# Cross-attention block on one core: context products in half-array pairs, the first norm in two chunks, the last first-pair queries after the values

## The chip, the cores and the metric

The kernel runs on one core of one Trainium2 chip. The metric is the device time of one execution in microseconds, as the median of several runs. Five engines work side by side, each with its own instruction queue: TensorE (PE; its weight loads are listed as PEld), VectorE (DVE), ScalarE (ACT), GpSimd (POOL) and SyncE (SP, which here only issues transfers). Semaphores order them.

## What is computed

```python
x: (4, 1024, 256)   ctx: (4, 64, 192)   HEADS, DHEAD, INNER = 16, 64, 1024   FF_HID = 1024
h = _ln(x, g1, be1)
x = _attn(h, h, Wq1, Wk1, Wv1, Wo1, bo1) + x
h = _ln(x, g2, be2)
x = _attn(h, ctx, Wq2, Wk2, Wv2, Wo2, bo2) + x
h = _ln(x, g3, be3)
y = h @ Wp + bp
a, gate = y[..., :FF_HID], y[..., FF_HID:]
out = a * gelu(gate) @ W2 + b2 + x
```

`_ln` is a normalization of each row by its mean and variance, then a scale g and a shift b. `_attn` is softmax attention with 16 heads and a scale of 1/8. All is float32.

## The kernel before

The code writes each engine's program by hand, in order; each instruction waits for semaphores that the other engines raise. No scheduler moves anything.

**The long part.** 64 steps C, each one pair of heads and one chunk of 512 queries: scores (L509, L513), exponential on ScalarE (L1161), sums of probabilities on GpSimd (L1406), values times probabilities (L526), and between them the next step's first scores (L483) with their maxima on VectorE (L833). Behind it come the cross-attention and the feed-forward part. None of it is touched, but everything must wait for the opening.

**The opening**, up to the first score at 62.26 us, in TensorE's order:

1. small matmuls that keep it busy (`rouse`), and the context turned by four transposes (`context_turn`);
2. 16 context products (L401), n = 0 to 15: eight for the cross keys, eight for the cross values, each for one pair of heads. The context has 192 features, so each product is two matmuls: 128 features, and the remaining 64, which are padded with zeros to 128 partitions (VectorE's memsets, L954 and L955). Six banks of PSUM (`CTX_BANKS`) go round; ScalarE copies each product out (L1114);
3. Wq2 turned (L414), copied out half by ScalarE (L1119) and half by VectorE (L819);
4. the first 512 rows of the first norm turned, `turn_norm((1, 0))` (L362);
5. eight key folds (`fold_keys`, L428), one for each pair of heads, each four matmuls with 64 rows of weights; VectorE (L812) and ScalarE (L1125) copy one head each; three pairs of banks go round;
6. the second 512 rows turned, `turn_norm((1, 1))`;
7. four projections of the first pair of heads (L457): u = 0 and 1 are keys of the first and second 512 rows, u = 2 and 3 queries of these; ScalarE (L1142) and VectorE (L827) split each into a high and a low part;
8. eight value folds (`fold_values`, L444), with two first scores behind each, copied by ScalarE (L1134);
9. eight value projections (L469), the transpose of the maxima (L493), and two projections of the second pair of heads.

**The first norm.** VectorE takes the statistics of eight tiles of 128 rows (L743, L745) once x is there; ScalarE takes the root (L1054), queued between its copies of products 11 and 12; VectorE inverts it (L753) and writes four tiles of normalized rows into `xn` (L764), copies its half of the turned Wq2, and writes the other four tiles when TensorE has turned the first. A chunk is turned in two halves k = 0, 1, through banks T0 and T1. ScalarE reads each half twice: into `hT`, rounded (L1102), and back into the bank in full (L1106); VectorE subtracts the two (L794), which frees the bank.

**Transfers.** SyncE issues all of them in one queue: context, weights Wk2 and Wv2 in four pieces of two transfers (L1564, L1565), x (L1525), Wq2 (L1567), the first pair's weights (L1530), six small vectors (L1570), then Wo2 and the rest.

## Time and profile before

| | us |
|---|---|
| median of 3 runs | 2023.52 (2023.45 to 2024.98) |
| the profiled execution | 2023.83 |
| its span | 2022.0 |
| PE busy | 2015.6 (100%) |
| GpSimd busy | 1476.4 (73%) |
| VectorE busy | 1390.4 (69%) |
| ScalarE busy | 1187.8 (59%) |
| first score of the long part starts | 62.26 |

The span runs from the first instruction to the last; the execution's own time has 1.8 us more around it. A timeline row gives start, time, engine, line, operation, what is written and read, and how many instructions are merged in it. A float32 matmul stands in the records as two instructions, so 16 records are 8 matmuls. TensorE's records overlap: one is listed some tenths of a us longer than the distance to the next.

### The profile page before, as it was taken

Reading aid. Unit: us, or ns where it says so; the run is one execution under the profiler, and the core shown is the slowest. Engines: PE = TensorE matmul, PEld = TensorE weight load, DVE = VectorE, ACT = ScalarE, POOL = GpSimd, SP = SyncE. Lnnn points to the kernel's source line nnn. Section 1 sums busy time; section 2 is a strip of 40 time slices with the busy share of each in tenths; the row PEclk is TensorE's granted clock in tenths of the full one; section 3 lists DMA queues with packets and bytes.
Section 4 is the critical chain, followed back from the end, with each engine's and each line's share of the span. In section 5 each row is a group of like instructions: output and inputs, shape, how many; then the busy total and the mean of one; then the engine's idle time right before and its main releaser. Section 6 shows DMA issues by size and latency. Waiting matters only on the chain.

```text
span 2022.0 us, 32384 instructions
## 1 busy us (share of the span) xinstructions
PE 2015.6 (100%) x12718; PEld 1386.8 (69%) x12718; DVE 1390.4 (69%) x2128; ACT 1187.8 (59%) x1895; POOL 1476.4 (73%) x785
## 2 busy tenths in 40 slices
PE   9999999999999999999999999999999999999999
PEld 8665665667565566765665666565558999888888
DVE  6587677666767785577678566758777888744443
ACT  6566576565557675565667555557665666533332
POOL 2699899978989998899899888989895576300000
PEclk9999999999999999999999999999999999999999
DMA  7300000001000000010000001000020520000100
GB/s 241 115 27 21 6 7 16 6 27 48 17 11 6 16 7 27 1 64 6 6 6 22 27 1 51 8 27 1 22 55 9 147 84 1 1 21 22 42 11 32
DMA packets 48183, 64.01 MB, mean 32 GB/s; under 512 B 6048, under 2 KB 41504, under 8 KB 46368
## 3 DMA queue, kind: packets, MB, share of 16 engines
q1 hardware_dynamic: 48032, 61.96, 9.7%
q8 instruction: 100, 1.64, 0.3%
q14 instruction: 51, 0.42, 0.1%
HBM read 43.07 MB, written 18.87 MB: 31 GB/s over the span
## 4 chain that ended last, share of the span: by engine, by line
PE 99%; ACT 0%; DMA 0%; issue 0%; DVE 0%; SPq 0%
PE score L526 22%; PE score L509 19%; PE score L652 9%; PE score L513 6%; PE score L457 5%; PE attn_project L637 5%; PE attn_project L666 5%; PE score L607 4%; PE attn_project L457 4%; PE first_score L483 4%; PE score L469 3%; PE score L575 2%; PE attn_project L575 2%; PE attn_project L483 2%; PE first_score L550 2%; PE attn_project L469 1%
## 5 line engine op out<-in xcount | busy, mean ns | idle before, releaser
L1406 POOL TENSOR_TENSOR acc<-acc,pT 128x1024 f32<-128x1024 f32 x384 | 916.9, 2388 | 53.8 <-POOL acc L1406 0.4
L1161 ACT ACTIVATE pT<-score 128x1024 f32<-128x1024 f32 x512 | 525.7, 1027 | 134.4 <-PE score L513 92.8
L509 PE MATMUL score<-qk 64*128 64x512 f32 x3072 | 456.6, 399 | 1.5 <-ACT oT L1174 0.9
L526 PE MATMUL score<-pT,vT 128*64 128x512 f32 x2016 | 446.5, 595 | 0.0
L833 DVE TENSOR_REDUCE nmax<-first_score 128x1 f32<-128x512 f32 x512 | 347.7, 679 | 4.8 <-PE first_score L483 2.9
L833 DVE TENSOR_REDUCE nmax<-attn_project 128x1 f32<-128x512 f32 x512 | 346.9, 678 | 0.0
L509 PEld LDWEIGHTS score<-qk 64*128 64x128 f32 x3072 | 257.3, 184 | 119.0 <-ACT pT L1161 67.9
L526 PEld LDWEIGHTS score<-pT,vT 128*64 128x64 f32 x2016 | 139.2, 137 | 289.4 <-issue 251.8
L855 DVE RECIPROCAL sums<-sums 128x512 f32<-128x512 f32 (+1 forms) x65 | 214.4, 3299 | 54.3 <-ACT sums L1207 53.7
L513 PE MATMUL score<-shift,pick 64*128 64x512 f32 x1024 | 205.5, 391 | 0.0
L483 PE MATMUL first_score<-qk 64*128 64x512 f32 x512 | 200.8, 392 | 0.0
L483 PE MATMUL attn_project<-qk 64*128 64x512 f32 x512 | 200.6, 392 | 0.0
L1403 POOL TENSOR_TENSOR acc<-pT 128x1024 f32<-128x1024 f32 x64 | 153.4, 2396 | 55.8 <-ACT pT L1161 55.8
L652 PE MATMUL score<-hT,wp 128*128 128x512 f32 x768 | 184.1, 396 | 0.0
L1393 POOL TENSOR_TENSOR xres<-xres,rows 128x1024 f32<-128x1024 f32 x8 | 19.2, 2399 | 203.1 <-DVE xn L764 203.1
L652 PEld LDWEIGHTS score<-hT,wp 128*128 128x128 f32 x768 | 142.3, 188 | 32.0
L1174 ACT COPY oT<-score 128x512 f32<-128x512 f32 x63 | 37.1, 588 | 212.1 <-PE score L526 211.9
L827 DVE SCALAR_TENSOR_TENSOR qk<-score,qk 128x512 fp32r<-128x512 f32 x67 | 46.1, 690 | 154.3 <-ACT qk L1142 154.3
L1207 ACT COPY sums<-first_score 32x512 f32<-32x512 f32 x248 | 143.1, 577 | 9.2 <-PE first_score L550 6.3
L1432 POOL TENSOR_TENSOR probs<-probs,rsum 128x1024 f32<-128x1024 f32 x32 | 61.0, 1906 | 90.8 <-DVE rsum L896 90.8
L848 DVE TENSOR_TENSOR shift<-first_score,mask 128x512 fp32r<-128x512 f32 x64 | 44.2, 691 | 116.9 <-PE first_score L493 116.9
L513 PEld LDWEIGHTS score<-shift,pick 64*128 64x128 f32 x1024 | 99.3, 184 | 21.2
(180 smaller groups left out, 3089.2 us busy)
## 6 DMA issues: line engine op xcount, KB each, us to landing
xres<-x_middle SPq DMA_DIRECT2D x10, 512.0 KB, 3.7
xres<-in_x SPq DMA_DIRECT2D x4, 1024.0 KB, 6.8
raw_qk<-in_L_xattn_Wq SPq DMA_DIRECT2D x32, 128.0 KB, 2.3
raw_qk<-in_L_xattn_Wk SPq DMA_DIRECT2D x32, 128.0 KB, 2.4
raw_v<-in_L_xattn_Wv SPq DMA_DIRECT2D x8, 512.0 KB, 3.9
keys_all<-keys SPq DMA_DIRECT2D x1, 4096.0 KB, 13.0
values_all<-values SPq DMA_DIRECT2D x1, 4096.0 KB, 12.4
out_x<-xres SPq DMA_DIRECT2D x7, 512.0 KB, 3.0
```

Of the source, the lines that this page charges most:

```text
L457: last = e.matmul(banks[bank], wqk[:, P % 2, w, kind, k, :], hT[:, h, k, c * BANK:(c + 1) * BANK], start=(i == k == 0), stop=(i == 2 and k ...
L483: last = e.matmul(banks[bank], qk[P % 2][r, w, q0:q0 + PART], qk[P % 2][r, 2 + h, half * BANK:(half + 1) * BANK], start=(m == 0), stop=(m ...
L509: e.matmul(bank, qk[P % 2][r, 2 + h, keys], qk[P % 2][r, w, queries], start=(part == 0), stop=False)
L513: e.matmul(bank, pick[r, :], shift[r, :], start=False, stop=True).then_inc(s.scored, 1)
L526: last = e.matmul(banks[bank][head * DH:(head + 1) * DH, :], vT[:, v_slot(D, jt), c0:c0 + DH], pT[:, jt, head, :], start=(jt == 0), stop=( ...
L652: last = e.matmul(banks[bank], wp[q][:, w, k, which, o:o + PART], hT[:, h, k, (c % 2) * BANK:(c % 2 + 1) * BANK], start=(term == k == 0), ...
L833: e.tensor_reduce(nmax[:, head, t, half:half + 1], banks[PASS_BANKS[head][half]], AX.X, ALU.max, negate=True).then_inc(s.row_max, 1)
L855: e.reciprocal(sums[:, C % 2, part], sums[:, C % 2, part]).then_inc(s.sum_inverse, len(halves))
L1161: e.activation(pT[:, jt].rearrange("p h n -> p (h n)"), SC[R % 2][:, :], ACT.Exp).then_inc(s.exponential, 1)
L1207: last = e.copy(sums[r * DH // 2:(r + 1) * DH // 2, o, :], banks[bank][g * DH // 2:(g + 1) * DH // 2, :])
L1403: e.tensor_tensor(total, pT[:, jt - 1], pT[:, jt], ALU.add).then_inc(s.probs_added, 1)
L1406: e.tensor_tensor(total, total, pT[:, jt], ALU.add).then_inc(s.probs_added, 1)
```

## The change

Three things, all in the opening.

**Context products in pairs.** The remaining 64 features of both keys' and values' weights are now loaded into two halves of the partitions (`wkv2_rest`: heads pairs 0 and 1 of each four on partitions 0 to 63, pairs 2 and 3 on 64 to 127). The turned context's remaining features are copied a second time, by ScalarE, to partitions 64 to 127. A group of four products makes four first parts and then four second parts with 64 rows each, which lie alternately in the lower and the upper half of the array. The order of the pairs within four is 0, 2, 1, 3. VectorE's two memsets are gone.

**The first norm by chunks.** x is loaded in two halves, the first between Wk2 and Wv2, the second behind Wv2 and g1, be1, which are moved up. Each half has statistics, a root, an inverse and rows of its own. The first chunk is turned before the last group of products, the second before the fourth key fold.

**The last queries of the first pair** (u = 3) are projected behind the value projections and the turned maxima, through another bank.

```diff
@@ the order of products @@
+        CTX_ORDER = [(i, TPC * half + p) for i in range(2) for half in range(PAIRS // TPC) for p in (0, 2, 1, 3)]
+        ctx_of = numbered(CTX_ORDER)
@@ TensorE @@
-            def context_product(n):
...
-                for k in range(2):
-                    last = e.matmul(banks[bank][:, 0:B * M], wkv2[:, i, k, p * PART:(p + 1) * PART], ctxT[:, k, :, :],
-                                    start=(k == 0), stop=(k == 1))
+            def context_products(g):
+
                 need.wait_ge(s.ctx_copied, 4)
-                need.wait_ge(s.padded, 2)
...
+                need.wait_ge(s.ctx_copied_a, 2)
+                need.wait_ge(wkv2_loaded[g], 32)
+                for n in range(4 * g, 4 * g + 4):
+                    i, p = CTX_ORDER[n]
+                    bank = CTX_BANKS[n % 6]
+                    bank_free(bank)
+                    e.matmul(banks[bank][:, 0:B * M], wkv2[:, i, p * PART:(p + 1) * PART], ctxT[:, 0, :, :],
+                             start=True, stop=False)
+                for n in range(4 * g, 4 * g + 4):
+                    i, p = CTX_ORDER[n]
+                    bank = CTX_BANKS[n % 6]
+                    r = slice(n % 2 * CREST, (n % 2 + 1) * CREST)
+                    c = p // TPC * BANK // 2 + p % 2 * PART
+                    e.matmul(banks[bank][:, 0:B * M], wkv2_rest[r, i, c:c + PART], ctxT[r, 1, :, :],
+                             start=False, stop=True).then_inc(s.ctx_product, 1)
+                    free[bank] = ((s.kv2_a, n + 1),)
...
-            for n in range(2 * PAIRS):
-                context_product(n)
+            for g in range(4):
+                context_products(g)
+                if g == 2:
+                    turn_norm((1, 0))
             turn_wq2()
-            turn_norm((1, 0))
             for p in range(PAIRS):
+                if p == 3:
+                    turn_norm((1, 1))
                 fold_keys(p)
-            turn_norm((1, 1))
-            for u, bank in zip((0, 2, 1, 3), CTX_BANKS):
+            for u, bank in zip((0, 2, 1), CTX_BANKS):
                 project_qk(0, u, bank)
...
             turn_max(0, "T1")
+            project_qk(0, 3, "PJ")
@@ VectorE @@
-            e.memset(wkv2[CREST:PART, :, 1, :], 0.0).then_inc(s.padded, 1)
-            e.memset(ctxT[CREST:PART, 1, :, :], 0.0).then_inc(s.padded, 1)
             context_turn()
-            for t in range(TILES):
+            for t in range(TPC):
                 stats1(0, t)
-            ln_inverse(rs1[:, :], (1, 0))
+            ln_inverse(rs1[:, 0:TPC], (1, 0))
             norm1(0)
+            for t in range(TPC, TILES):
+                stats1(0, t)
+            turn_half((1, 0), 0, "T0")
+            ln_inverse(rs1[:, TPC:], (1, B))
+            norm1(1)
             turn_wq2()
-            norm1(1)
             for p in range(PAIRS):
                 fold_keys(p)
-                if p == 3:
-                    turn_norm((1, 0))
+                if p == 1:
+                    turn_half((1, 0), 1, "T1")
             turn_norm((1, 1))
...
             make_shift(0, "T1")
+            split_qk(0, 3, "PJ")
@@ ScalarE @@
+            def context_turn():
+
+                bpt = PART // M
+                for a in range(2):
+
+                    need.wait_ge(s.ctx_copied, 2 * a + 2)
+                    e.copy(ctxT[CREST:PART, 1, a * bpt:(a + 1) * bpt, :],
+                           banks[TURN_BANKS[2 * a + 1]][0:CREST, 0:PART].rearrange("p (b m) -> p b m", b=bpt)
+                           ).then_inc(s.ctx_copied_a, 1)
...
+            context_turn()
             for n in range(2 * PAIRS):
                 context_product(n)
-                if n == TILES + 3:
-                    ln_root(mv1[:, :, 1], (1, 0), (1, TILES - 1))
+                if n == 5:
+                    ln_root(mv1[:, 0:TPC, 1], (1, 0), (1, TPC - 1))
+                if n == 11:
+                    turn_half((1, 0), 0, "T0")
+                if n == 13:
+                    ln_root(mv1[:, TPC:, 1], (1, B), (1, TILES - 1))
             turn_wq2()
+            turn_half((1, 0), 1, "T1")
             for p in range(PAIRS):
-                if p < KT:
-                    turn_half((1, 0), p, ("T0", "T1")[p])
+                if 4 <= p < 4 + KT:
+                    turn_half((1, 1), p - 4, ("T0", "T1")[p - 4])
                 fold_keys(p)
-            turn_norm((1, 1))
-            for u, bank in zip((0, 2, 1, 3), CTX_BANKS):
+            for u, bank in zip((0, 2, 1), CTX_BANKS):
                 split_qk(0, u, bank)
...
+            split_qk(0, 3, "PJ")
@@ GpSimd @@
-            need.wait_ge(*rows_there((1, 0)))
+            need.wait_ge(*rows_there((1, 1)))
             split_wqk(0)
-            need.wait_ge(*rows_there((1, 1)))
             split_wv(0)
@@ SyncE @@
-                    e.dma_start(wkv2[:, i, 0, part], w[0:PART, part]).then_inc(there, 16)
-                    e.dma_start(wkv2[0:CREST, i, 1, part], w[PART:CD, part]).then_inc(there, 16)
-            load_x(0)
+                    rest = slice(half * INNER // 4, (half + 1) * INNER // 4)
+                    e.dma_start(wkv2[:, i, part], w[0:PART, part]).then_inc(there, 16)
+                    e.dma_start(wkv2_rest[:, i, rest], w[PART:CD, part].rearrange("r (g n) -> g r n", g=2)
+                                ).then_inc(there, 16)
+                if i == 0:
+                    load_x_first(0)
+            for c, v in enumerate((g1, be1)):
+                load_cols(c, v, s.cols1_loaded)
+            load_x_first(1)
             e.dma_start(wq2[:, :, :], Wq2.rearrange("(k p) n -> p k n", p=PART)).then_inc(s.wq2_loaded, 16)
             load_wqk(0)
```

How rows move. First TensorE, from the first context product to the first key folds. Before:

```order
L401 MATMUL score0<-ctxT,wkv2 128x256 x4
L401 MATMUL score1<-ctxT,wkv2 128x256 x4
L414 MATMUL attn_project<-ident,wq2 128x128 x8
L414 MATMUL score0<-ident,wq2 128x128 x8
L362 MATMUL first_score<-ident,xn 128x128 x8
L428 MATMUL score0<-kv2,wq2T 128x256 x4
L428 MATMUL score1<-kv2,wq2T 128x256 x4
L428 MATMUL attn_project<-kv2,wq2T 128x256 x4
```

And in the changed kernel, from the third group of products on:

```order
L409 MATMUL score1<-ctxT,wkv2 128x256 x2
L409 MATMUL attn_project<-ctxT,wkv2 128x256 x2
L416 MATMUL score1<-ctxT,wkv2_rest 128x256 x2
L416 MATMUL attn_project<-ctxT,wkv2_rest 128x256 x2
L369 MATMUL first_score<-ident,xn 128x128 x8
L409 MATMUL score0<-ctxT,wkv2 128x256 x2
L409 MATMUL score1<-ctxT,wkv2 128x256 x2
L416 MATMUL score0<-ctxT,wkv2_rest 128x256 x2
L416 MATMUL score1<-ctxT,wkv2_rest 128x256 x2
L428 MATMUL attn_project<-ident,wq2 128x128 x8
L428 MATMUL score0<-ident,wq2 128x128 x8
L442 MATMUL score0<-kv2,wq2T 128x256 x4
```

The turn of the norm's rows (`first_score<-ident,xn`) moved from between Wq2's turn and the key folds to before the last group.

Second VectorE, from the end of the statistics to the first key copies. Before:

```order
L753 RECIPROCAL rs<-sd 128x8
L764 TENSOR_SCALAR xn<-xres,mv,rs 128x256 x4
L819 COPY wq2T<-attn_project 128x4x128
L819 COPY wq2T<-score 128x4x128
L764 TENSOR_SCALAR xn<-xres,mv,rs 128x256 x4
L812 TENSOR_SCALAR keys<-score 128x8x64 x2
```

In the changed kernel:

```order
L814 TENSOR_TENSOR hT<-first_score,hT 128x512
L773 RECIPROCAL rs<-sd 128x4
L784 TENSOR_SCALAR xn<-xres,mv,rs 128x256 x4
L839 COPY wq2T<-attn_project 128x4x128
L839 COPY wq2T<-score 128x4x128
L832 TENSOR_SCALAR keys<-score 128x8x64 x2
L814 TENSOR_TENSOR hT<-first_score,hT 128x512
```

The copies of the turned Wq2 now stand behind the rows of the second chunk, and these behind the second inverse.

Third ScalarE, from the copies of the last products to the projections' first splits. Before:

```order
L1054 ACTIVATE sd<-mv,eps 128x8
L1114 COPY kv<-score 128x256 x4
L1119 COPY wq2T<-attn_project 128x4x128
L1119 COPY wq2T<-score 128x4x128
L1102 ACTIVATE hT<-first_score,cols 128x512
L1106 ACTIVATE first_score<-first_score,cols 128x512
L1125 ACTIVATE keys<-score 128x8x64
L1102 ACTIVATE hT<-first_score,cols 128x512
L1106 ACTIVATE first_score<-first_score,cols 128x512
```

In the changed kernel:

```order
L1148 COPY kv<-score 128x256 x2
L1076 ACTIVATE sd<-mv,eps 128x4
L1148 COPY kv<-score 128x256 x2
L1153 COPY wq2T<-attn_project 128x4x128
L1153 COPY wq2T<-score 128x4x128
L1125 ACTIVATE hT<-first_score,cols 128x512
L1129 ACTIVATE first_score<-first_score,cols 128x512
L1159 ACTIVATE keys<-score 128x8x64 x2
L1159 ACTIVATE keys<-attn_project 128x8x64
L1159 ACTIVATE keys<-score 128x8x64
L1125 ACTIVATE hT<-first_score,cols 128x512
L1129 ACTIVATE first_score<-first_score,cols 128x512
```

The root of the second chunk stands two product copies later than the one root before, and the two halves of a chunk's turn now stand among the later key copies.

## Rows read from the trace of the kernel before

**Rows 1.** The page: busy time, and the chain that ended last.

```profile
PE 2015.6 (100%) x12718; PEld 1386.8 (69%) x12718; DVE 1390.4 (69%) x2128; ACT 1187.8 (59%) x1895; POOL 1476.4 (73%) x785
...
PE 99%; ACT 0%; DMA 0%; issue 0%; DVE 0%; SPq 0%
```

**Rows 2.** Stretches: us, each engine's busy us, granted clock, DMA share, GB/s.

```profile
30.00:35.00 5.00, 4.25 (x25) 3.08 (x21) 2.47 (x5) 4.67 (x8) 5.00 (x8) 1.00 0.74 315
...
100.00:125.00 25.00, 25.00 (x164) 14.90 (x164) 19.34 (x26) 17.63 (x24) 23.91 (x12) 1.00 0.04 11
```

**Rows 3.** Timeline (start, time, engine, line, what): TensorE's products, Wq2's turn, value projections.

```profile
5.42 4.37 PE L401 MATMUL score<-ctxT,wkv 128*128 128x256 f32 x16 [0.22 <-DMA wkv<-in_L_xattn_Wk]
...
9.63 1.89 PE L401 MATMUL attn_project<-ctxT,wkv 128*128 128x256 f32 x8
...
19.99 1.04 PE L414 MATMUL attn_project<-ident,wq 128*128 128x128 f32 x8
...
47.96 11.46 PE L469 MATMUL score<-wv,hT 128*128 128x512 f32 x48
```

**Rows 4.** Timeline: TensorE at changes between whole-array and half-array matmuls.

```profile
27.59 1.06 PE L428 MATMUL attn_project<-kv,wq2T 64*128 64x256 f32 x8
...
28.46 1.92 PE L428 MATMUL score<-kv,wq2T 64*128 64x256 f32 x16
...
30.31 0.86 PEld L362 LDWEIGHTS first_score<-ident,xn 128*128 128x128 f32 x8 [0.33 <-issue]
30.31 1.09 PE L362 MATMUL first_score<-ident,xn 128*128 128x128 f32 x8
...
34.95 3.05 PE L457 MATMUL score<-hT,wqk 128*128 128x512 f32 x12 [0.75 <-issue]
...
37.93 1.13 PE L444 MATMUL score<-wo,kv 64*128 64x256 f32 x8
```

**Rows 5.** Timeline: from the root to the first key fold.

```profile
18.14 0.30 ACT L1054 ACTIVATE sd<-mv,eps 128x8 f32<-128x8 f32 x1 [1.03 <-DVE mv L745]
...
18.35 0.63 ACT L1114 COPY kv<-score 128x256 f32<-128x256 f32 x2
...
18.47 0.20 DVE L753 RECIPROCAL rs<-sd 128x8 f32<-128x8 f32 x1 [0.37 <-ACT sd L1054]
...
18.71 1.38 DVE L764 TENSOR_SCALAR xn<-xres,mv,rs 128x256 f32<-128x256 f32 x4
...
21.94 0.69 DVE L819 COPY wq2T<-score 128x512 f32<-128x512 f32 x1 [0.18 <-PE score L414]
...
22.78 2.00 PE L428 MATMUL score<-kv,wq2T 64*128 64x256 f32 x16
```

**Rows 6.** Timeline: ScalarE's turns and key copies, the last split, the second value fold.

```profile
22.38 0.78 ACT L1102 ACTIVATE hT<-first_score,cols 128x512 fp32r<-128x512 f32 x1 [0.29 <-PE first_score L362]
...
23.19 0.75 ACT L1106 ACTIVATE first_score<-first_score,cols 128x512 f32<-128x512 f32 x1
...
26.40 0.60 ACT L1125 ACTIVATE keys<-attn_project 128x512 f32<-128x512 f32 x1
...
26.88 0.61 ACT L1125 ACTIVATE keys<-score 128x512 f32<-128x512 f32 x1
...
36.63 0.60 ACT L1142 ACTIVATE qk<-score 128x512 fp32r<-128x512 f32 x1 [1.57 <-PE score L457]
...
37.27 0.69 DVE L827 SCALAR_TENSOR_TENSOR qk<-score,qk 128x512 fp32r<-128x512 f32 x1 [1.22 <-ACT qk L1142]
...
39.50 1.10 PE L444 MATMUL score<-wo,kv 64*128 64x256 f32 x7 [0.20 <-DVE qk L827]
```

**Rows 7.** Timeline of x and Wq2; last a transfer issue: count, KB, us to landing.

```profile
6.42 0.74 SPq L1567 DMA_DIRECT2D wq<-in_L_xattn_Wq  x1
...
13.77 0.43 DVE L743 BATCH_NORM_STATS2 stats<-xres 128x6 f32<-128x256 f32 x1 [9.08 <-DMA xres<-in_x]
...
wq<-in_L_xattn_Wq SPq DMA_DIRECT2D x1, 1024.0 KB, 10.0
```

More of the change, by code:

```diff
@@ L422, in fold_keys @@
                 need.wait_ge(s.wq2T_in_v, KT)
-                need.wait_ge(s.kv2_a, p + 1)
+                need.wait_ge(s.kv2_a, ctx_of[0, p])
                 bank_free(*fold_banks(p))
@@ L440, in fold_values @@
                     p = 2 * half + o
-                    need.wait_ge(s.kv2_a, PAIRS + p + 1)
+                    need.wait_ge(s.kv2_a, ctx_of[1, p])
                     for head, bank in enumerate(fold_banks(n % 2)):
@@ L747, in stats1 @@
             def stats1(b, t):
-                need.wait_ge(x_loaded[b % 2], 16 * (b // 2 + 1))
+                if b == 0 and t < TPC:
+                    need.wait_ge(s.x_first_loaded, 16)
+                else:
+                    need.wait_ge(x_loaded[b % 2], 16 * (b // 2 + 1))
                 ln_stats(xres[:, b % 2, t, :], mv1[:, t, :], (1, TILES * b + t))
@@ L786, in turn_half @@
                 if (key, k) in full_v:
-                    need.wait_ge(s.cols_loaded, 96)
+                    need.wait_ge(s.cols_loaded, 64)
                     which = key[0] - 1
@@ L1056, in norm_rows @@
             def norm_rows(key, src, rs, t0):
-                need.wait_ge(s.ln_negated, root_of[key[0], key[1] // CHUNKS] - 1 if key[0] == 1 else B)
+                need.wait_ge(s.ln_negated, key[1] // CHUNKS if key[0] == 1 else B)
                 need.wait_ge(s.ln_rstd, root_of[key[0], key[1] // CHUNKS])
@@ L1099, in turn_half @@
                 need.wait_ge(s.ln_turned, turned_by(key, k))
-                need.wait_ge(s.cols_loaded, 96)
+                need.wait_ge(s.cols1_loaded, 32)
+                need.wait_ge(s.cols_loaded, 64 if which else 0)
                 hT_free(key)
```

41 lines of the change are left out of this document (22 added, 19 removed).

## The prediction

> **What bounds the kernel now.** I read the busy times of the page first: TensorE is busy for 2015.6 of the span of 2022.0 us, and the chain that ended last is 99% PE [rows 1]. So an edit pays only where TensorE itself does less or waits less. The stretches show where it waits. In the long loop it doesn't, though GpSimd is nearly full there; in the opening it waits 0.75 us of one stretch [rows 2]. The diff touches only the opening, up to the first exponential at about 62 us, so the timeline of 0 to 50 us is what the sum is made from. What comes after is moved as a block. The loop has no idle time that could grow or shrink with a shift of a few us, and I cost it at nothing; if that cover is false, the price is the last rival below.
>
> The times that follow are on the clock of the profiled run. I rebuild when things happen in the new order and compare them with the old ones at two points: the first key fold (22.78 us before) and the second value fold, `fold_values(1)` (39.50 us before) [rows 5, 6].
>
> **Context products.** Between 9.63 and 19.99 us TensorE makes 12 products of two matmuls: 10.36 / 24 = 0.43 us each [rows 3]. A key fold is four matmuls with 64 rows of weights and as many columns, and starts 0.87 us after the one before it (27.59 to 28.46) [rows 4]. They run two at a time, at 0.22 us each. The eight pairs of second parts so save 8 x 0.43 = 3.46 us.
>
> Against that stands the change between whole-array and half-array matmuls, which before happens once after the products and now happens twice in each of four groups. Going in: 12 projection matmuls start at 34.95 and the value fold starts at 37.93, 2.98 us later, where 12 at the pitch of the 48 value matmuls ((11.46 - 0.16) / 48 = 0.235 us; a record ends 0.16 after the next one starts) are 2.83; the 0.15 left, with 0.07 in a slow first matmul (1.13 against 1.06 us), is 0.2 us. Going out: the sixteen records from 28.46 end their slots at 30.19 and the transposes start at 30.31, and last 1.09 instead of 1.04 us: 0.17 us [rows 3, 4]. So I take 0.37 us a group. The bounds are 0 and 0.66 (twice the 0.33 us that the weight load sat idle before 30.31 us [rows 4]); I stay with the middle value because both directions have a row of their own. A group costs 1.73 + 0.87 + 0.37 = 2.97 us instead of 3.46, and four save 2.0 us, not 3.46.
>
> The Trainium skill, "TensorEngine Tiling (Array Packing)", section Tiling Modes (Key Properties), says that changing the tiling mode drains TensorE. The overview of that page speaks of up to twice the speed for contractions of 64 or less. By the second alone the products would save 3.46 us; the rows side with the first.
>
> The first 16 records need 4.21 us where 16 need 3.46: the first three run at the lower clock [rows 3]. That costs 0.75 us and stays. The start stays at 5.42, which a weight transfer sets. ScalarE's two new copies of the turned context follow VectorE's; a 128x256 copy takes 0.37 us, and TensorE has its small warming matmuls meanwhile, so between 0 and 0.3 us are at stake; I take 0. The removed memsets of VectorE lay beside the context's loading and give nothing.
>
> So the groups end at 9.15, 12.1 and 15.1 us; the turn of norm (1, 0) follows (8 transposes, 0.88 us); the last group runs from 15.96 to 18.93; the turn of Wq2 ends at 20.7.
>
> **Are inputs there in time?** Before, all rows of x had landed at 13.77, and Wq2, issued at 6.42, 10.0 us later at 16.4 [rows 7]. Now half of x goes between the weights. From 0.5 MB in a stream of about 0.27 MB a us (1 MB of x in the 3.7 us after the weights) it costs 1.9 us of queue, so this half lands near 8.6, the second near 14.3 and Wq2 near 17.0. Four tiles' statistics take half of the 4.33 us that eight take up to 18.10: first half 10.8, second 16.5. The first half's root stands behind the copy of product 5 (12.2), its rows are ready near 14.2, 0.9 us before TensorE asks for them. Nothing waits for a transfer. SyncE queues two small g1/be1 loads ahead of Wq2, 1 us each to issue; that is in the numbers.
>
> **The new wait.** The second root is placed behind the copy of product 13 on ScalarE. That product is in the last group's first pair, done at 15.96 + 1.73 + 0.2 + 0.43, plus 0.22 to the copy = 18.54; two copies at 0.32 and the root starts at 19.17. From there before's own rows give the rest: reciprocal 0.33 later, rows 0.57 later, 1.38 long, two copies of the turned Wq2 on VectorE of 0.69, and 0.15 to TensorE [rows 5]. 19.17 + 0.57 + 1.38 + 1.38 + 0.15 = **22.65 us** for the first key fold. Before it was 22.78. TensorE is done at 20.7 and stands for 2.0 us: VectorE turns Wq2 only after it has written the second chunk's rows. Before, it wrote the first chunk's rows (18.71) there, and the second chunk's behind the copies. The queued victims are both VectorE copies and the second ScalarE half behind them. So the 2.0 us saved in the products are given back whole here, all but **0.13 us**.
>
> **From the fold to `fold_values(1)`.** Three folds end at 25.25. The turn (1, 1) is then split: its second half needs T1, which VectorE frees after two key copies (24.6 to 25.3) and a subtraction of 0.69, at 26.1. Its price is 0.3 us, plus 0.37 for changing tiles. Folds 3 to 6 run from 26.7 to 30.2. On ScalarE the turn's two halves (0.78 + 0.75, 1.57 us with gaps [rows 6]) now stand between keys 3, 4 and 5: keys 4 end at 30.5 and hold up fold 7 by 0.5 us (to 31.5). The three key copies behind them follow at 0.48 us, and free the bank of the first queries at 33.15, 0.1 after TensorE. Three projections at 1.40 end at 36.1. ScalarE's split starts 0.2 later, VectorE's 0.64 after that (36.63 to 37.27) and lasts 0.69; TensorE starts 0.14 behind it: 37.8 for `fold_values(1)` [rows 6]. Before: 39.50. What left is the stall of 0.75 us for the second chunk's turn [rows 4], the second chunk's transposes ahead of the projections (0.88, now inside the folds), and one projection (1.40). What came are the stalls above. The gain here is 1.7 us.
>
> **The fourth projection.** It is made behind the values, and costs its 1.40 us there; VectorE, idle then, hides its split. 1.7 - 1.40 = **0.3 us** at the main loop's start. Between these points the eight value folds and first scores keep their pace: they and their copies are unchanged. SyncE stores the cross keys some 2 us later (they end at 33.6 instead of about 31), still before the values' store; they have landed by about 47, the exponentials begin at 61.
>
> **Sum.** The profiled execution took 2023.83 us (span 2022.0, 1.8 around it). 2023.8 - 0.3 = 2023.5. The median shown is 2023.52, 0.3 under the profiled time, so against it the forecast is 2023.2 us.
>
> **Rivals.**
> 1. The changes of tile cost nothing. The group is 2.6 us, product 13 comes 3 x 0.37 + 0.2 = 1.3 us earlier, and so does the fold; 0.3 more goes in the folds. Gain 1.9 us, 2021.6. For it: TensorE's queue could load weights over the boundary. Against it: both boundaries show a gap [rows 4]. With every small wait of the fold stage gone too, 2020.8.
> 2. The second parts don't pair. The groups cost 0.87 more, product 13 comes 3 x 0.87 + 0.43 = 3.0 us later, **2026.2, slower**. It decides if even one of each pair waits for the other. Against it: the folds have the same alternation and are paired throughout.
> 3. The 2.0 us wait lets TensorE's clock fall. In the opening its records reach the 2.4 GHz pitch only with the fourth after 5.42, near 6.8 us (5.42 + 0.75 + 3 x 0.22) [rows 3]. If the folds had to repeat all of that, some 6 us at 1.2 GHz would cost half of them, 3.0 us: 2026.2, slower. It decides once 2.0 us of waiting is enough for the clock to fall. Against: after the gap ending at 34.95 the records are at full pitch at once [rows 4]. No row shows a gap of 2 us. The Trainium skill, "TensorE: Matmul & The Clock Gate", Part 1, says that throttled is the default state and that activity releases it; the rows of the first matmuls agree.
> 4. A transfer is late. The second half of x has 2.6 us of slack before the root, the first 0.9. Beyond that each us costs one: 2024 to 2026.
> 5. The main loop reacts to the shift, with GpSimd 96% busy in one stretch [rows 2] and first weights arriving relatively earlier; either sign, by up to 5 us.
>
> **How the numbers follow.** Forecast 2023.2 with 0.62 (own range 2022.4 to 2024.2, the upper end being tile changes of 0.66 a group). Rival 1: 0.18. Rival 2: 0.05. Rival 3: 0.05. Rival 4: 0.05. Rival 5: 0.05. The range 2020.8 to 2025.8 holds the first, rival 1, most of rival 4 and part of 5. 0.2% is 4.05 us, about what a measurement of this kernel can tell from no change; none of the first four reaches it in either direction. Same 0.92, faster 0.04, slower 0.04.
>
> **What would show it.** Right: context groups 2.9 to 3.0 us apart, half-row matmuls starting in pairs; a root near 19.2; a TensorE gap of about 2 us before the first key fold near 22.6; `fold_values(1)` near 37.8; the first score of the loop near 62.0 instead of 62.26. Wrong: a first key fold before 21.5 or after 24 us, or a loop of another length.

## The result, and the profile after

| | before | changed |
|---|---|---|
| median, us (17 runs of each, side by side) | 2025.07 (2022.95 to 2025.64) | 2027.72 (2027.28 to 2028.16) |
| the profiled execution | 2023.83 | 2027.69 |
| its span | 2022.0 | 2025.9 |

The ratio is 1.0016 [1.0009, 1.0022]: slower, by about as much as a measurement of this kernel can tell. The forecast was 2023.2, with a range up to 2025.8. The times of the kernel before fall into two groups some 2 us apart (2023.0 to 2024.0 and 2024.9 to 2026.1), so its median says mostly how many of each it caught; those of the changed kernel lie within 0.9 us. From here on I compare profiled executions, point by point. The two differ by 3.9 us.

The page of the changed kernel, against [rows 1]: TensorE has less to do, and the span is longer.

```profile
span 2025.9 us, 32389 instructions
...
PE 2014.7 (99%) x12718; PEld 1383.0 (68%) x12718; DVE 1388.9 (69%) x2127; ACT 1187.5 (59%) x1898; POOL 1477.2 (73%) x785
```

TensorE's busy time fell by 0.9 us; the rest of the span, in which it waits, rose from 6.4 to 11.2 us. The loss is in waits. Next the timeline of TensorE in the opening of the changed kernel, the answer to [rows 3 to 5] (columns as there; the bracket is the idle time before the row, and what ended it).

```profile
8.14 3.59 PE L409 MATMUL score<-ctxT,wkv 128*128 128x256 f32 x8 [3.14 <-DMA wkv_rest<-in_L_xattn_Wk]
11.66 1.13 PE L416 MATMUL score<-ctxT,wkv_rest 64*128 64x256 f32 x8
...
16.37 1.13 PE L409 MATMUL score<-ctxT,wkv 128*128 128x256 f32 x4 [0.58 <-DMA wkv_rest<-in_L_xattn_Wv]
...
19.36 1.09 PE L369 MATMUL first_score<-ident,xn 128*128 128x128 f32 x8
...
24.27 1.09 PE L428 MATMUL attn_project<-ident,wq 128*128 128x128 f32 x8 [1.01 <-DMA wq<-in_L_xattn_Wq]
...
27.25 2.00 PE L442 MATMUL score<-kv,wq2T 64*128 64x256 f32 x16 [1.02 <-DVE wq2T L839]
```

The first product starts at 8.14, where it started at 5.42 [rows 3]; three of the four brackets name a weight transfer. The rows of VectorE and ScalarE on the way to the second root, against [rows 5, 7]:

```profile
21.59 0.43 DVE L760 BATCH_NORM_STATS2 stats<-xres 128x6 f32<-128x256 f32 x1 [3.73 <-DMA xres<-in_x]
...
22.86 0.65 ACT L1148 COPY kv<-score 128x256 f32<-128x256 f32 x2 [0.65 <-PE score L416]
...
23.85 0.30 ACT L1076 ACTIVATE sd<-mv,eps 128x4 f32<-128x4 f32 x1 [0.35 <-DVE mv L762]
...
24.53 1.38 DVE L784 TENSOR_SCALAR xn<-xres,mv,rs 128x256 f32<-128x256 f32 x4
...
25.83 0.59 ACT L1153 COPY wq2T<-score 128x512 f32<-128x512 f32 x1 [0.28 <-PE score L428]
...
26.43 0.68 DVE L839 COPY wq2T<-score 128x512 f32<-128x512 f32 x1
```

VectorE stood 3.73 us for the second half of x, which was there at 21.6; the root waited for these statistics and not, as forecast, for a product's copy. From the root on the chain is the forecast one: 0.68 to the rows, 1.30 and 0.60 to the second copy, 0.82 to the fold at 27.25.

That wait is the last of three that end close together. The copies of products 12 and 13, behind which the root stands, ended at 23.51, so the root waited only 0.35 us for its statistics: the last group itself started at 20.29 where I had 15.96, as the group before it stood until 16.37 for its weights. And the turn of Wq2 stood until 24.27 for Wq2; ScalarE could copy its second half at 25.83. With x alone in time I estimate a fold 0.35 us earlier, by that wait. It was not one transfer that came late but several.

Why did x come so late? SyncE's row of issues (start, time that the issue took):

```profile
7.10 3.17 SPq L1614 DMA_DIRECT2D wkv<-in_L_xattn_Wv  x1
...
11.12 2.95 SPq L1573 DMA_DIRECT2D cols<-in_L_xattn_g  x1
...
14.81 0.66 SPq L1569 DMA_DIRECT2D xres<-in_x  x1
```

Two issues took 3 us each, where most take 0.4 to 1.6. The second half of x was issued at 14.81, half a microsecond after the time at which I had it landed. Meanwhile the 16 DMA engines had little to do. Stretches (columns as in [rows 2]):

```profile
8.00:10.00 2.00, 1.86 (x5) 1.53 (x6) 0.00 (x0) 0.00 (x0) 0.00 (x0) 0.51 0.59 196
10.00:12.00 2.00, 2.00 (x9) 1.30 (x9) 0.00 (x0) 0.00 (x0) 0.00 (x0) 0.64 0.43 159
12.00:14.00 2.00, 2.00 (x14) 1.52 (x11) 1.05 (x5) 1.20 (x4) 0.00 (x0) 1.00 0.15 51
14.00:16.00 2.00, 1.79 (x12) 0.98 (x10) 1.04 (x5) 0.61 (x3) 0.00 (x0) 1.00 0.25 48
```

The last two rows have a DMA share of 0.15 and 0.25 and some 50 GB/s, with megabytes waiting to be issued. The first two show a second thing, the granted clock at 0.51 and 0.64: TensorE fell to its lower level (1.2 GHz) at 8.0 us, and had the upper one (2.4 GHz) back at 11.45.

So there were two suspects. **Transfers**: from 13.0 us on, while a load of `wkv2_rest` runs, the trace has 23 and 24 packets of 1 KB in half a microsecond, of 47 ns each, and next to none of another transfer: 24 x 0.047 / 0.5 is the work of 2.3 engines. Such a load of 128 packets takes 128 x 0.047 / 2 = 3 us (an estimate, if two engines carry it), and four of them 12 us if it is the same two. The first and the third group wait for one, the third until 16.37 for a load issued at 6.52; SyncE's issues behind them are held up; and the first half of x, issued at 3.51, was there only 9.3 us later. **Clock**: TensorE, left idle for 3.1 us, fell to half speed, and the first group took 3.52 us for its first parts instead of 1.9.

### The profile page after: what moved, and what is told of

The parts are those of the page before. It is cut to its first block, busy times and chain, and to the rows that moved or that the text cites. A ratio compares the mean times of both kernels' runs of the same rounds, so it can differ in the third digit from the quotient of the medians.

```text
span 2025.9 us, 32389 instructions
## 1 busy us (share of the span) xinstructions
PE 2014.7 (99%) x12718; PEld 1383.0 (68%) x12718; DVE 1388.9 (69%) x2127; ACT 1187.5 (59%) x1898; POOL 1477.2 (73%) x785
## 4 chain that ended last, share of the span: by engine, by line
PE 98%; SPq 1%; ACT 0%; DMA 0%; DVE 0%; issue 0%
PE score L540 22%; PE score L523 18%; PE score L666 9%; PE score L527 6%; PE score L471 5%; PE attn_project L651 5%; PE attn_project L680 5%; PE score L621 4%; PE first_score L497 4%; PE attn_project L471 4%; PE score L483 3%; PE score L589 2%; PE attn_project L589 2%; PE attn_project L497 2%; PE first_score L564 2%; PE attn_project L483 1%
```

## The experiments

The checkpoints of every profiled execution, in us from the span's start. "Clock up" is when the records go over to the pitch of the upper level; before the first rise the records of the same matmul follow at twice the distance (0.43 instead of 0.22 us). From the loop's first score to the end it is 1959.5 to 1959.9 us in every kernel, so the loop's start says all.

| kernel | clock up | first product | first key fold | `fold_values(1)` | loop | span | ratio to before |
|---|---|---|---|---|---|---|---|
| before | 6.81 | 5.42 | 22.78 | 39.50 | 62.26 | 2022.0 | |
| before, again | 5.16 | 5.63 | 22.30 | 39.01 | 61.78 | 2021.4 | one run |
| changed | 4.62 (fell at 8.0, up again 11.45) | 8.14 | 27.25 | 42.05 | 66.23 | 2025.9 | 1.0016 |
| a_spread | 5.55 | 6.67 | 22.90 | 37.69 | 61.87 | 2021.5 | 0.9997 |
| a_rouse | up throughout | 8.01 | 27.38 | 42.18 | 66.36 | 2026.1 | 1.0015 |
| b_two | 10.56 | 7.53 | 30.42 | 47.43 | 70.20 | 2029.9 | 1.0035 |
| b_three | 9.10 | 5.79 | 24.09 | 40.80 | 63.56 | 2023.0 | 1.0006 |
| b_one | 4.96 (fell at 8.4, up again 15.20) | 9.33 | 37.71 | 54.41 | 77.18 | 2037.0 | one run |
| a_spread_wq | 4.54 | 6.81 | 22.41 | 37.19 | 61.37 | 2021.1 | 0.9998 |
| a_spread_u3 | 10.55 | 5.84 | 24.35 | 40.63 | 63.41 | 2023.0 | 1.0002 |
| b_u3 | 9.19 | 5.69 | 24.09 | 39.30 | 63.48 | 2023.1 | 0.9997 |
| a_inorder | 10.21 | 5.56 | 24.21 | 39.02 | 63.19 | 2022.9 | 0.9999 |
| a_best | 6.37 | 5.20 | 21.50 | 36.29 | 60.46 | 2020.1 | 0.9993 |

### The same data over all DMA engines (a_spread)

```diff
-                    rest = slice(half * INNER // 4, (half + 1) * INNER // 4)
                     e.dma_start(wkv2[:, i, part], w[0:PART, part]).then_inc(there, 16)
-                    e.dma_start(wkv2_rest[:, i, rest], w[PART:CD, part].rearrange("r (g n) -> g r n", g=2)
-                                ).then_inc(there, 16)
+                    if half == 0:
+                        for g in range(2):
+                            e.dma_start(wkv2_rest[g * CREST:(g + 1) * CREST, i, :].rearrange("r (h n) -> r h n", h=2),
+                                        w[PART:CD].rearrange("r (h g n) -> g r h n", h=2, g=2)[g]).then_inc(there, 16)
```

As many transfers and bytes as in the changed kernel; each now has 64 rows as its outermost size instead of 2, in packets of the same 1 KB. Both loads of a weight's rest now come with its first half, and TensorE's waits count them so.

> The changed kernel with one thing altered: the remaining 64 rows of Wk2 (and of Wv2) come in two transfers with 64 partitions outermost (each both column halves) instead of two transfers whose outermost size is 2; bytes and number of transfers are the same. Theory T (a transfer with an outermost size of 2 runs on two of the 16 DMA engines, so the first products wait for it and SyncE's queue is held up behind it): the first product starts near 6.0 us instead of 8.14, the second half of x is issued near 8 instead of 14.81 us, the first key fold starts near 23 instead of 27.25 us, fold_values(1) 14.8 us later, the first score of the loop near 62 instead of 66.23, span 2021.5 to 2022.5, 4 us under the changed kernel's 2025.9. Rival R (x's first half among the weights is what delays them): the first product stays at or after 7.5 us and the span above 2025. Rival C (the clock that fell at 8.0 us costs it): gain of at most 1.7 us.

Median 2023.36, ratio 0.9997 [0.9988, 1.0006]; span 2021.5, 4.4 us under the changed kernel's. The timeline and the stretches of a_spread:

```profile
6.67 1.97 PE L409 MATMUL score<-ctxT,wkv 128*128 128x256 f32 x8 [1.45 <-DMA wkv_rest<-in_L_xattn_Wk]
8.56 1.14 PE L416 MATMUL score<-ctxT,wkv_rest 64*128 64x256 f32 x8
...
16.53 1.89 PE L409 MATMUL score<-ctxT,wkv 128*128 128x256 f32 x8
18.36 1.13 PE L416 MATMUL score<-ctxT,wkv_rest 64*128 64x256 f32 x8
...
22.90 2.00 PE L442 MATMUL score<-kv,wq2T 64*128 64x256 f32 x16 [1.51 <-DVE wq2T L839]
```

```profile
12.00:14.00 2.00, 2.00 (x14) 1.51 (x11) 1.48 (x7) 1.38 (x5) 0.00 (x0) 1.00 1.04 364
14.00:16.00 2.00, 2.00 (x15) 1.28 (x14) 1.93 (x8) 0.73 (x3) 0.00 (x0) 1.00 1.04 385
```

Where the changed kernel moved 51 and 48 GB/s, this one moves 364 and 385. The second half of x is issued at 8.03 instead of 14.81, and the first is there 6.8 us after its issue instead of 9.3. The whole loss is gone with the shape of the load. What is left is an opening that goes as forecast (next section). This edit removes the fallen clock too, so it doesn't yet tell the suspects apart.

### Only the clock kept up (a_rouse)

```diff
-            rouse(3)
+            rouse(30)
```

> The changed kernel with 30 small warming matmuls instead of 3 between the context's turn and the first product, so that TensorE doesn't stand still while the weights are on their way and its clock needn't fall; the transfers are the changed kernel's own. Theory T: the first group of products is 1.7 us shorter (its first parts 1.8 instead of 3.5 us), but the first key fold still waits for the second half of x, which lands at 21.6 us, so it stays near 27.2 and the span within 0.5 us of 2025.9. Rival C (the clock costs the time): the first key fold is 1.7 us earlier and the span near 2024.2.

Median 2027.80, ratio 1.0015 [1.0006, 1.0024]: nothing gained.

```profile
8.01 1.97 PE L409 MATMUL score<-ctxT,wkv 128*128 128x256 f32 x8
...
16.25 1.13 PE L409 MATMUL score<-ctxT,wkv 128*128 128x256 f32 x4 [1.67 <-DMA wkv_rest<-in_L_xattn_Wv]
...
21.71 0.43 DVE L760 BATCH_NORM_STATS2 stats<-xres 128x6 f32<-128x256 f32 x1 [4.76 <-DMA xres<-in_x]
```

The small matmuls bridged the gap, and the first group ran at full pitch (1.97 instead of 3.59 us). What it gained was waited away at the next loads: the third group stood 1.67 us instead of 0.58 for its weights and started at 16.25 (16.37 in the changed kernel), and VectorE stood 4.76 instead of 3.73 us for the second half of x, which came at 21.7 as before. The clock fell in the changed kernel, and it cost nothing at the end. The transfers decide.

### The suspected shape put into the kernel before (b_two, b_three, b_one)

The rest of each weight is loaded in two pieces, of 62 and 2 rows; in the control of 48 and 16; and in the third of 61 and 3. The number of transfers and of bytes is the same in all three.

```diff
-                    e.dma_start(wkv2[0:CREST, i, 1, part], w[PART:CD, part]).then_inc(there, 16)
+                    for r in (slice(0, CREST - 2), slice(CREST - 2, CREST)):
+                        e.dma_start(wkv2[r, i, 1, part], w[PART + r.start:PART + r.stop, part]).then_inc(there, 16)
```

(with `CREST - 16` and `CREST - 3` in the other two)

> The kernel before with the remaining 64 rows of each weight quarter loaded in two transfers of 62 and 2 rows instead of one of 64. 62 is divisible by 2 and by no other number up to 16. Theory T (the number of DMA engines follows the outermost size): both run on two engines; 62 packets of 2 KB on two engines at about 0.09 us each are 2.8 us, so the first product starts 2 to 3 us later than 5.42, x lands 3 us or more after 13.77, SyncE's issues are held up, and the span grows by 2 to 4 us over 2022.0. Rival (only bytes and the number of transfers count): like the control with 48 and 16 rows.

> Control to the run with 62 and 2 rows: the same kernel and the same number of transfers, but of 48 and 16 rows, both divisible by 16. Theory T: 16 engines each, the first product within 0.3 us of 5.42; four more issues of 0.5 us put x and Wq2 some 2 us later in the queue, of which at most 0.5 us reaches the first key fold (22.78), span 2021.8 to 2022.8. Rival (the number of transfers is what costs): like the run with 62 and 2 rows, within 0.5 us.

> As the run with 62 and 2 rows, but with 61 and 3 rows: 61 has no divisor up to 16 but 1. Theory T (the number of engines is the largest divisor up to 16 of the outermost size): one engine takes 61 packets of 2 KB at 0.09 us, 5.5 us for each quarter, so the first product starts near 9 us instead of 7.53 and the first key fold 8 us or more after b_two's 30.4, span 2036 or more. Rival (any odd shape costs about the same): within 1 us of b_two.

b_two: median 2031.48, ratio 1.0035 [1.0021, 1.0048]. b_three: 2025.01, 1.0006 [0.9996, 1.0015]. b_one: 2038.81 in one run. Here is b_two, its start, an issue of SyncE, a stretch, and the wait of the statistics (engine, line, what it waited for: us in total, times, longest):

```profile
7.53 5.18 PE L401 MATMUL score<-ctxT,wkv 128*128 128x256 f32 x16 [2.27 <-DMA wkv<-in_L_xattn_Wk]
```

```profile
9.00 5.63 SPq L1568 DMA_DIRECT2D wq<-in_L_xattn_Wq  x1
```

```profile
8.00:10.00 2.00, 2.00 (x6) 1.55 (x6) 0.00 (x0) 0.37 (x1) 0.00 (x0) 1.00 0.23 66
```

```profile
DVE stats L743 <- DMA xres<-in_x: 17.4, 1, 17.4
```

Then the control b_three, the start and the same wait:

```profile
5.79 5.32 PE L401 MATMUL score<-ctxT,wkv 128*128 128x256 f32 x16 [0.53 <-DMA wkv<-in_L_xattn_Wk]
```

```profile
DVE stats L743 <- DMA xres<-in_x: 9.8, 1, 9.8
```

And b_one, with a stretch from its first products:

```profile
9.33 6.59 PE L401 MATMUL score<-ctxT,wkv 128*128 128x256 f32 x16 [4.15 <-DMA wkv<-in_L_xattn_Wk]
```

```profile
DVE stats L743 <- DMA xres<-in_x: 25.3, 1, 25.3
```

```profile
9.00:11.00 2.00, 1.67 (x4) 1.44 (x5) 0.00 (x0) 0.00 (x0) 0.00 (x0) 0.50 0.06 25
```

The same rows cut at 62 instead of 48 bring back the signs of the changed kernel: a first product that waits for its weights, an issue of 5.63 us that begins in a stretch with a DMA share of 0.23 and 66 GB/s, and x late by 7.6 us. Between 9.0 and 9.5 us b_two moves 12 packets, of 2 KB and 85 ns each: 12 x 0.085 / 0.5 is the work of 2.0 engines. In the control, with sizes that 16 divides, the first product is 0.37 us later than before and x 0.7 us. A long issue alone is not the sign: the control has one too (2.86 us at 10.95), and a_spread one of 2.70 at 15.12, but the DMA share over them is 1.03 and 1.15, where it is 0.71 over b_two's and 0.67 and 0.33 over the changed kernel's two.

Most of what x lost in b_two is not in its issue. It was issued at 8.56, 1.7 us after the control's 6.87, but took 13.6 us to land instead of 7.6. A likely reason is that x, as a transfer over all engines, has its part on the two that are behind as well; this is argued and not shown, as the trace doesn't tell the engines apart.

In b_one the DMA share is 0.06, which is one engine of 16, at 25 GB/s; the first product waits until 9.33, and VectorE for x for 25.3 us. The fold came 7.3 us after b_two's, where at least 8 were expected. (In b_two and b_one the clock falls later too, at 27.6 and 28.9 us, as TensorE waits for x and weights, so part of their +7.9 and +15 us is that.) The control's first fold, 1.3 us after that of before, has two parts: a start 0.37 later, and 0.95 in the first 16 records, 5.32 us against 4.37 [rows 3], for which b_again, below, has a reason.

The Trainium skill, "DMA: Bandwidth & Descriptors", section "Why a DMA increments its semaphore by 16 and not by 1", says that the slowest dimension whose size isn't 1, of source and of destination, sets how many of the 16 engines take part: the largest number up to 16 that divides both. By it the changed load (outermost 2 at the source) has two engines, 62 rows two, 61 rows one, 48 and 16 rows sixteen. The DMA share of 0.15 in the changed kernel, the 2.0 engines' work in b_two, the share of 0.06 in b_one and the nearly undelayed control agree. It was there to be read, and I didn't hold the new load's shape against it.

### The kernel before once more (b_again)

No edit; one more profile, because the rise of the clock seemed to differ from run to run.

> The kernel before, unchanged, once more with a profile. Its times fall into two groups about 2 us apart (2023.1 to 2023.9 and 2025.0 to 2026.1), those of the changed kernel into one 0.9 us wide. Theory P (TensorE's clock comes up at another moment from run to run, and the kernel before has its products on the critical chain from the start): the span is 2022.0 plus half of what the clock comes up later than 6.8 us, and everything after the last context product keeps its distances. Rival (something in the long loop): the distance from the first score to the end differs from 1959.8.

It took 2023.2 us (span 2021.4). The first 16 records of the products, in b_again and in b_u3 (below), which up to there is the same program:

```profile
5.63 3.69 PE L401 MATMUL score<-ctxT,wkv 128*128 128x256 f32 x16 [0.43 <-DMA wkv<-in_L_xattn_Wk]
```

```profile
5.69 5.42 PE L401 MATMUL score<-ctxT,wkv 128*128 128x256 f32 x16 [0.46 <-DMA wkv<-in_L_xattn_Wk]
```

3.69, 4.37 [rows 3] and 5.42 us for the same records: the clock rises at 5.16, 6.81 and 9.19 us. In a kernel whose products are on the chain this moves the end by up to 1.7 us. From the first product to the first key fold, less half of the time that the products ran at the lower level, it is 16.65 to 16.67 us in before, b_again, b_three and b_u3. This is the likely cause of the two groups of times; I have profiles with early and late rises, but not enough to show that each execution of the upper group had the late one. The changed kernel waits for x either way, which fits its narrow times.

The distances in the next four experiments are corrected in this way, for start and clock.

### The queries alone (b_u3), and all but the queries (a_spread_u3)

The kernel before, with the third part of the change alone, on all three engines:

```diff
-            for u, bank in zip((0, 2, 1, 3), CTX_BANKS):
+            for u, bank in zip((0, 2, 1), CTX_BANKS):
                 project_qk(0, u, bank)
...
             turn_max(0, "T1")
+            project_qk(0, 3, "PJ")
```

> The kernel before with only the last queries' projection moved behind the value projections and the turned maxima. Theory T: fold_values(1) near 38.0 instead of 39.50, the first score of the loop at 62.15 plus or minus 0.2 against 62.26. Rival: the loop starts at 61.5 or earlier.

a_spread with the same edit undone:

> The run a_spread with the fourth projection of the first pair (its last queries) back in its old place, ahead of the value folds. Theory T (the projection costs its 1.4 us in either place): fold_values(1) starts near 39.2 instead of 37.69, the first score of the loop at 61.9 plus or minus 0.2, as in a_spread. Rival (moving it wins by starting the row maxima earlier): the loop starts 0.8 us or more later than in a_spread.

b_u3: median 2024.81, ratio 0.9997 [0.9988, 1.0007]. a_spread_u3: 2024.81, 1.0002 [0.9993, 1.0011]. Both times are of no use by themselves, since the clock rose late in both profiles. The distances are: from the first fold to `fold_values(1)` 15.21 in b_u3 against 16.71 before, so 1.50 less; from there to the loop 24.18 against 22.76, so 1.42 more. Moving the queries is worth 0.1 us. In a_spread_u3 the first distance is 16.28: the norm by chunks takes 0.43 us out of the fold stage. With start and clock as in a_spread, its loop would have begun at 63.41 + 0.83 - 2.35 = 61.9, as a_spread's did.

### VectorE's copies of Wq2 ahead of the second chunk's rows (a_spread_wq)

```diff
             ln_inverse(rs1[:, TPC:], (1, B))
-            norm1(1)
             turn_wq2()
+            norm1(1)
```

> The run a_spread with one move on VectorE: the two copies of the turned Wq2 stand ahead of the second chunk's rows instead of behind them. In a_spread TensorE has finished the turn at 21.3 us and the first key fold starts at 22.90, held by those copies. Theory T (this order makes the wait): the fold starts near 22.3, the rows end near 23.6, still before TensorE asks for them, and the first score of the loop comes 0.5 us earlier, at 61.4, span 21.0 over 2000. Rival (the late rows only move the wait to the second chunk's turn): fold 22.3, but the loop's start unchanged at 61.9.

Median 2024.22 against 2024.94, ratio 0.9998 [0.999, 1.0007].

```profile
22.41 2.00 PE L442 MATMUL score<-kv,wq2T 64*128 64x256 f32 x16 [0.88 <-DVE wq2T L839]
```

The fold starts 16.23 - 15.60 = 0.6 us earlier after the first product, and the loop 55.20 - 54.56 = 0.6. The wait that the forecast spoke of is on the chain, at the place that it named, and this takes most of it away.

### The products' order undone (a_inorder)

a_spread with the pairs of a group in the order 0, 1, 2, 3, so that two second parts for the lower half of the array follow each other, and then two for the upper.

```diff
-        CTX_ORDER = [(i, TPC * half + p) for i in range(2) for half in range(PAIRS // TPC) for p in (0, 2, 1, 3)]
+        CTX_ORDER = [(i, TPC * half + p) for i in range(2) for half in range(PAIRS // TPC) for p in (0, 1, 2, 3)]
...
-                    r = slice(n % 2 * CREST, (n % 2 + 1) * CREST)
+                    r = slice(n // 2 % 2 * CREST, (n // 2 % 2 + 1) * CREST)
```

> The run a_spread with the four second parts of a group in the order lower, lower, upper, upper half of the array instead of lower, upper, lower, upper (the pairs of heads are taken 0, 1, 2, 3). Theory Q (only neighbours in the queue overlap, so the alternating order is what makes pairs): the second and third part overlap, the others stand alone, a group is 0.43 us longer, the last group's first pair later too, and the distance from the first product to the first key fold is 1.3 to 1.7 us over a_spread's 16.2 at full clock. Rival (the queue finds the pairs itself): 16.2 plus or minus 0.2.

Median 2024.60, ratio 0.9999 [0.999, 1.0008].

```profile
12.69 0.48 PE L416 MATMUL attn_project<-ctxT,wkv_rest 64*128 64x256 f32 x1
12.70 0.48 PE L416 MATMUL score<-ctxT,wkv_rest 64*128 64x256 f32 x1
13.01 0.38 PE L416 MATMUL attn_project<-ctxT,wkv_rest 64*128 64x256 f32 x1
13.02 0.38 PE L416 MATMUL score<-ctxT,wkv_rest 64*128 64x256 f32 x1
```

My theory, that pairs need the alternating order, fell. The matmuls start in twos, 0.01 us apart. One of each two goes to `attn_project`, where products 4 and 5 lie, the other to `score`, where 6 and 7 lie, so the two are not neighbours in the program. A group costs the same, and the corrected distance to the fold is 16.33 against 16.23. The order 0, 2, 1, 3 is worth 0.1 us at most.

### The best of it (a_best)

a_spread_wq, with the rest of Wk2 in four transfers of 64 rows, two for each half, so that less stands ahead of the first group. That of Wv2 stays in two, and TensorE's waits count the transfers of each group.

```diff
+                    if i == 0:
+                        for g in range(2):
+                            c = half * INNER // 2 + g * INNER // 4
+                            e.dma_start(wkv2_rest[g * CREST:(g + 1) * CREST, i, half * INNER // 4:(half + 1) * INNER // 4],
+                                        w[PART:CD, c:c + INNER // 4]).then_inc(there, 16)
```

> The changed kernel with both corrections: the remaining rows of Wk2 in four transfers of 64 partitions and one column half each, those of Wv2 in two, all with 64 partitions outermost, and VectorE's copies of the turned Wq2 ahead of the second chunk's rows. Theory T: the first product starts near 5.8 us instead of 6.8 (only 0.38 MB of weights stand before it, not 0.51), the first key fold 15.6 us later at 21.4, fold_values(1) 14.8 and the loop 24.2 after that: first score at 60.4 if TensorE's clock is up at the first product, and half a us more for each us it comes up later; span 2020.1 against 2021.4 of the kernel before under the same condition, a gain of 1.3 us. Rival (a transfer or the first half's rows become late by the earlier start): first key fold no earlier than 22.0 us.

Median 2022.77 (11 runs) against 2025.22, ratio 0.9993 [0.9984, 1.0002]; span 2020.1, the shortest of all.

```profile
5.20 2.55 PE L409 MATMUL score<-ctxT,wkv 128*128 128x256 f32 x8
...
60.46 0.96 PE L523 MATMUL score<-qk 64*128 64x512 f32 x6
```

Nothing waits for the first weights (no bracket), and the loop starts at 60.46, 1.8 us before the kernel before did, and 1.3 us before b_again, whose clock rose 1.2 us earlier than here. The runs alone don't separate it from before: the interval reaches 1.0002.

## Why the prediction was wrong

**What bounds the kernel: right.** The loop and all behind it take 1959.7 us in every kernel, whether it starts at 60.5 or at 77.2 us. Rival 5, a loop that reacts to the shift, is false.

**Context products: right.** A group was to cost 2.97 us. At full clock in a_spread it costs 2.96 (9.63 us there is the second group's start, 6.67 the first's), 2.99 and 2.98, and the last 2.89 (16.53 to 19.42). The price of changing tiles, 0.37 us a group, was the right size. With that rivals 1 (changes of tile free: 2.6) and 2 (no pairs: 3.8) are both out.

**"The start stays at 5.42, which a weight transfer sets": wrong.** It named the very row that would move, and then didn't cost the new transfer. It is 8.14 in the changed kernel; in a_spread, with no slow transfer, 6.67, because a third transfer stands ahead of the first group; in a_best 5.20. ScalarE's copies, on which I put 0 to 0.3 us, play no part where a transfer ends the wait; in a_best the second ends at 5.05, 0.15 us ahead of the first product, and may set it.

**"Are inputs there in time?": the step that failed.** It gave the new loads their bytes in a stream of 0.27 MB/us and concluded that nothing waits for a transfer. For transfers over 16 engines bytes were a fair measure: in a_spread Wq2 is issued at 8.54 and lands 8.7 us later, at 17.2, where I had 17.0, the second half of x is there by 14.7 (14.3), the first at 10.5 (8.6, at no cost to TensorE). A 128 KB load on two engines runs at 128 / 3 = 43 KB/us, a sixth of that stream (both estimates from the packets), and what it blocks is more than itself: SyncE's next issues stand 3 us, and what lies behind it lands late. The forecast had the second half of x landing at 14.3; it was there at 21.6.

**Rival 4 was the case, and its price rule held, in part by luck.** It said 2.6 us of slack, and from there one us lost for each. 21.6 - 14.3 - 2.6 = 4.7 us; the second root came at 23.85 instead of 19.17, 4.7 late, the fold at 27.25 instead of 22.65, 4.6 late. What was wrong was its size (2024 to 2026, so 0.8 to 2.8 us beyond the slack) and its chance of 0.05, both taken from landings over 16 engines. By its own rule a transfer 7.3 us late gives 2023.2 + 4.7 = 2027.9. The luck is that the rule prices one late transfer with the rest in time: the products and Wq2 were 4.3 and 4.0 us late as well (20.29 - 15.96; 25.83 + 0.82 - 22.65) and stayed just behind x.

**The clock (rival 3): did not happen where I looked, did where I didn't.** The wait ahead of the folds is 1.51 us in a_spread and 1.02 in the changed kernel, and the folds run at full pitch. The fall came in the 3.14 us ahead of the first product, a wait that the forecast didn't have, and a_rouse shows that it was hidden behind the transfers.

**The new wait: right in place, 0.2 long in size.** In a_spread the second root is at 19.62 (forecast 19.17; the start is 1.25 us later than assumed, and the 0.75 us of slow records that I let stand are not there, as the clock rose before the start), and the fold follows 3.28 us later, not 3.48: the second copy of Wq2 follows after 0.60, not 0.69. TensorE stands 1.5 us (forecast 2.0).

**From the fold to `fold_values(1)`: right within 0.4.** Forecast 15.15, measured 14.8 in the changed kernel and in a_spread; 16.7 before. **The fourth projection: right.** Forecast 1.40, measured 1.42.

Two rows of the changed kernel close the account: `fold_values(1)` and the loop's start.

```profile
42.05 1.13 PE L458 MATMUL score<-wo,kv 64*128 64x256 f32 x8
...
66.23 0.96 PE L523 MATMUL score<-qk 64*128 64x512 f32 x6
```

Against before, +2.72 us at the first product, +1.75 more up to the first fold, -1.92 to `fold_values(1)`, +1.42 to the loop: +3.97, and the two executions differ by 3.9. Of these the first two were to be -0.13 together and are +4.47, of which a_spread takes back 4.35 (27.25 - 22.90) by the shape of the loads alone; the last two were to be -0.17 together (15.15 - 16.72 + 1.40), and are -0.50.

So the stretches that the forecast had worked out from rows came out within 0.5 us each. The one that it took over from the old kernel without a look at the new instruction's shape cost 4.4. That a_spread's profiled execution took 2023.36, against a forecast of 2023.5 on that clock, is partly luck: its first product was 1.25 us late, and the early clock gave 0.75 back. With the clock up early the kernel before took 2023.20 (b_again), so a_spread gained nothing against it: from the first product to the loop it needs 55.20 instead of 56.15 us, and its first product starts 1.04 us later.

## What to carry to other kernels

Cost a new transfer by its shape before its bytes: look at the outermost size of both sides, and if 16 doesn't divide it, reckon the bytes over fewer engines, and add what it does to everything behind it in the same queue, which may be issued late and may land late. A low DMA share with a long issue on the queue is the sign of it in a profile; a long issue at a full DMA share is not. When two suspected causes appear in one trace (here a late transfer and a fallen clock), remove each alone: the more striking of them may be hidden behind the other.

## What was unexpected of the hardware

- **A transfer on two engines holds up what is queued behind it.** Issues behind it took 3.17 and 2.95 us in the changed kernel and 5.63 in b_two, where most take 0.4 to 1.6, with the DMA share at 0.15 to 0.25 in part of each. A transfer of all engines behind it lands late besides: x took 13.6 us in b_two and 7.6 in the control.
- **The clock's first rise comes at another time in each execution**: at 4.5 to 10.6 us for openings that are nearly the same, with the small warming matmuls at the same place. The granted clock reads 1.00 before the first rise as well (the records of the products are 0.43 us apart there and 0.22 after it), so the rise is to be read from the distance of the records. In the kernel before it is worth up to 1.7 us.
- **The fall.** Granted clock 0.5 came in waits of 3.14 us (changed kernel) and 4.15 (b_one), and in b_two behind two waits of 1.41 and 1.36 us with 1 us of work between them; in b_one it came once more, 1.4 us after the end of a wait of 2.85. Single waits of 1.51 us (a_spread, ahead of the folds) and 1.80 us (a_spread_wq, ahead of the first product) passed without one.
- **Half-array matmuls pair by themselves** when their order in the program doesn't alternate (a_inorder).
